# Attention loop of a fused convolution and attention kernel: the projection ahead before the transposes on PE, its conversion before the probabilities' copy on ACT

## What is computed

```python
q = hidden_states @ Wq                        # hidden_states: 8 images, 256 tokens, 128
k, v = jnp.split(hidden_states @ Wkv, 2, axis=-1)
scores = jnp.einsum('bqhd,bkhd->bhqk', q * scale, k).astype(jnp.bfloat16)
probs = jax.nn.softmax(scores, axis=-1)
out = jnp.einsum('bhqk,bkhd->bqhd', probs.astype(jnp.float32), v)
out = out.astype(jnp.bfloat16)
return out.reshape(B, S, H * dh).astype(jnp.float32) @ Wo + bo
```

## Time and profile before

| what | value |
|---|---|
| time, median of 3 runs | 681.39 us (680.37 to 681.64) |
| the profiled execution's own time | 678.21 us |
| its span on the core | 676.3 us |
| the changed loop | from about 376 to 508 us of the span |
| PE, DVE, ACT busy over the span | 91%, 80%, 59% |
| copy_out to copy_out, images 1 to 5 | 15.82 us each |

### The profile page before, as it was taken

The page is one execution under the profiler, slowest core; times in us unless marked ns, Lnnn a source line. Parts: engine busy times, 40 slices in busy tenths (PEclk is TensorE's granted clock), DMA queues, the critical chain, the costliest instruction groups (busy, mean ns, idle before and its releaser), DMA issues. The chain is left out here.

```text
span 676.3 us, 10078 instructions
## 1 busy us (share of the span) xinstructions
PE 614.9 (91%) x3226; PEld 486.4 (72%) x3226; DVE 541.3 (80%) x1150; ACT 401.6 (59%) x787; POOL 148.0 (22%) x114
## 2 busy tenths in 40 slices
PE   6998987997899999999997899999857799999996
PEld 4784665885678888887886778777746578888784
DVE  2638479975778778878788799999969589999986
ACT  3522221003678888888884799899953545555552
POOL 0095055754511001111011121111103011111200
PEclk9699586998899999999999555555558889999998
DMA  4000000002042211221000000000001232222200
GB/s 178 1 0 1 0 1 0 1 1 64 7 153 93 95 33 61 93 93 54 9 1 0 1 2 1 0 0 0 1 0 47 86 109 79 103 82 88 95 33 31
DMA packets 9699, 28.78 MB, mean 43 GB/s; under 512 B 960, under 2 KB 3264, under 8 KB 9536
## 3 DMA queue, kind: packets, MB, share of 16 engines
q1 hardware_dynamic: 9664, 28.34, 12.1%
HBM read 27.15 MB, written 1.18 MB: 42 GB/s over the span
## 5 line engine op out<-in xcount | busy, mean ns | idle before, releaser
L1249 DVE TENSOR_TENSOR hL<-hraw,hH 128x1024 fp32r<-128x1024 f32 (+1 forms) x128 | 131.1, 1050 | 35.9 <-ACT hH L1009 35.2
L1083 PE MATMUL ps<-xH,wH 128*128 128x512 f32 x256 | 103.7, 405 | 1.8 <-DVE xL L1154 1.1
L1013 ACT ACTIVATE hraw<-ps,bias 128x512 f32<-128x512 f32 x128 | 86.5, 685 | 28.8 <-PE ps L1085 24.4
L1085 PE MATMUL ps<-xH,wL 128*128 128x512 f32 x256 | 102.8, 402 | 0.0
L1084 PE MATMUL ps<-xL,wH 128*128 128x512 f32 x256 | 102.8, 401 | 0.0
L944 POOL TENSOR_TENSOR wL<-wraw,wH 128x1024 fp32r<-128x1024 f32 (+1 forms) x16 | 36.4, 2274 | 237.6 <-DVE wH L1135 237.6
L1097 PE MATMUL ps<-hH,wH 128*128 128x512 f32 x192 | 76.5, 398 | 7.5 <-DVE hL L1249 7.5
L1099 PE MATMUL ps<-hH,wL 128*128 128x512 f32 x192 | 76.2, 397 | 0.0
L1098 PE MATMUL ps<-hL,wH 128*128 128x512 f32 x192 | 75.9, 395 | 0.0
L1018 ACT ACTIVATE hraw<-ps 128x512 f32<-128x512 f32 x64 | 38.3, 599 | 52.0 <-PE ps L1085 50.4
L1009 ACT ACTIVATE hH<-hraw 128x1024 fp32r<-128x1024 f32 x64 | 67.5, 1055 | 1.0
(11 more groups left out here) (238 smaller groups left out, 1210.6 us busy)
## 6 DMA issues: line engine op xcount, KB each, us to landing
G<-gates_scratch SPq DMA_DIRECT2D x32, 512.0 KB, 4.7
wraw<-in_ex SPq DMA_DIRECT2D x8, 514.5 KB, 5.8
wraw<-in_ex SPq DMA_DIRECT2D x8, 384.0 KB, 5.1
w<-in_pack SPq DMA_DIRECT2D x1, 1420.5 KB, 8.1
xs<-in_x SPq DMA_DIRECT2D x4, 256.0 KB, 4.7
out<-acc SPq DMA_DIRECT2D x4, 256.0 KB, 2.1
w<-in_pack SPq DMA_DIRECT2D x1, 501.0 KB, 3.7
gates_scratch<-gT SPq DMA_DIRECT2D x4, 32.0 KB
```

The lines of the kernel that those rows point to most:

```text
L1013: act.activation(hraw[:, k % 2, h, :], ps[:, h, :], ACT.Gelu, bias=bias[:, place(k, last)[0], h:h + 1]).then_inc(z["act"], 1)
L1083: pe.matmul(o, wH[:, p, at:at + P], xa, start=True, stop=False)
L1085: x = pe.matmul(o, wL[:, p, at:at + P], xa, start=False, stop=True)
L1249: dve.tensor_tensor(hL[:, k % 2, g * half:(g + 1) * half, :], src, hi.bitcast(F32), ALU.subtract).then_inc(z["hl"], 1)
```

## The change

On PE, `project` now stands before `transposed` in each step; on ACT, `upper` now stands before `evacuate`. What is issued, and every wait, stays as it was.

```diff
@@ -1408,10 +1408,10 @@
             def step(b, g, first):
                 if there(*ahead(b, g, 2)):
                     rounded(*ahead(b, g, 2))
+                if there(*fragment(b, g, 5)[:2]):
+                    upper(*fragment(b, g, 5))
                 if g != 3 and not (first and g == 0):
                     evacuate(*((b, g - 1) if g else (b - 1, 3)))
-                if there(*fragment(b, g, 5)[:2]):
-                    upper(*fragment(b, g, 5))
                 if there(*ahead(b, g, 1)):
                     exponentials(*ahead(b, g, 1))
@@ -1548,9 +1548,9 @@
                 if g == 2 and not first:
                     final(b - 1)
-                transposed(b, g)
                 if there(*fragment(b, g, 6)[:2]):
                     project(*fragment(b, g, 6))
+                transposed(b, g)
```

## The result

The changed kernel takes 688.2 us (median of 4 runs, 686.85 to 691.12), the kernel before 681.09 in the same comparison. The ratio is 1.0117, with a 95% interval of 1.0085 to 1.015: 8.0 us slower by the ratio, between 5.8 and 10.2, and 7.1 us between the two medians. The forecast was 687.5.

A forecast was written before the change was run, and what follows sets the result against it. DVE was taken to bound the looped images, and the new order to make a longer cycle. Image 0 (1.15), four periods (4.12) and a fifth (0.8) gave 6.1 us, on 681.39 making 687.5 us, range 684.4 to 690.

The forecast's parts named there:

- upper bound of 17.07: Looped images: longest period forecast, in us, with every possible register-row cost added to 16.45.
- the cycle: Looped images: chain from `copy_out` through `lower`, projection, transposes, ACT's copies and value product to `copy_out`, 16.85 us against 15.82.
- unknown part of the register rows: Late starts at the projection and PE's other value product: cost shown by no row, half of it taken, 0.21 us.
- What bounds the kernel before: Looped images: DVE sets the pace, with a period of 15.82 us filled by its own work.
- DVE's own stretch: DVE from `copy_out` to the end of the image's last `lower`: 8.46 us without a wait, durations as before.
- The register rows: PE's instructions between a wait and the first matmul: 0.19 us more at the looped value product, taken as certain.
- The beginning: Loop's start: `lower`'s 3.51 us wait shortens by 0.88 us, but late first copies spend that gain.
- 1.1 us of slack: Kernel before, from the transposes to DVE: lateness that the queues of ACT and PE could absorb, about 1.1 us.
- rival 1: Looped images: DVE stays the bound and the lateness is covered; 680.5 to 681.4 us, no change; chance 0.06.
- the clock stood at half in the loop: Against the rival that PE's clock returns to 2.4 GHz in the loop, giving 679 us; chance 0.05.
- the register rows cost less, not more, than was taken: Against the rival that some four late starts a period cost 0.4 us each, giving 690.5 to 693; chance 0.08.
- rival 4: Looped images: half covered, as DVE's own copy path takes up part of the lateness; 682.8 to 684.4 us; chance 0.04.

The follow-up runs named there:

- e4: Kernel before, with POOL's value split started after the division of two steps before the image, not after its first scores' rounding; ratio to before 0.9998.
- e5: Changed kernel, with `lower` ahead of `normalise` on DVE; ratio to the kernel before 1.0067.
- e6: Changed kernel, with `copy_out` on DVE moved behind `centre` in an image's third step; ratio to the kernel before 1.0055.
- e3: Changed kernel, with POOL's value split started after the division of two steps before the image, not after its first scores' rounding; ratio to the kernel before 1.0058.
- e1: Changed kernel with ACT's old order restored, so only PE's projection stands ahead of the transposes; ratio to the kernel before 1.0086.
- e2: Kernel before with only ACT's half of the change, the conversion ahead of the copy; ratio to before 1.0093.

## Why the prediction was right

The sign and the mechanism came out, and so did the size by the timed medians (+7.1 for +6.1). By the loop the forecast was too low: the periods of 17.18 to 17.30 us lie above its upper bound of 17.07, and 8.0 us above its 7.4. That the median of the changed kernel came within 0.7 us of 687.5 is in part luck, since its four runs go from 686.85 to 691.12. Two terms of the sum were off, in opposite directions. Along the cycle, with the times of the period shown above:

| piece | forecast | measured |
|---|---|---|
| DVE, `copy_out` to the end of the last `lower` | 8.46 | 430.45 + 0.42 - 421.75 = 9.12 |
| hand-over and projection | 0.06 + 0.91 | 431.74 - 430.87 = 0.87 |
| transposes and hand-over | 1.03 + 0.06 | 432.94 - 431.74 = 1.20 |
| ACT, copy to copy | 3.82 | 436.77 - 432.94 = 3.83 |
| copy, hand-over with register rows | 1.02 + 0.06 + 0.19 | 438.03 - 436.77 = 1.26 |
| value product | 0.60 | 438.63 - 438.03 = 0.60 |
| output's transposes, hand-over | 0.37 + 0.06 | 439.05 - 438.63 = 0.42 |
| unknown part of the register rows | 0.21 | none |
| sum | 16.85 | 17.30 |

- *What bounds the kernel before*: DVE, and it does; e4 shows it, where POOL's 0.47 us became 0.30 + 0.05 and the period 0.12 shorter.
- *The cycle*: apart from DVE's own stretch and the unknown part, each piece is within 0.11 us. That ACT's path from copy to copy is the one that counts, and not PE's beside it, held too: ACT reaches the second copy, at 436.77, without a wait. e5 and e6 each take a piece out of the cycle, and the period falls.
- *The register rows*: at the value product nearly all of the 0.19 us was there (the copy ends at 437.80, the product starts at 438.03, 0.23 us later). At the projection it was not: `lower` ended at 430.87 and the projection started at 430.93. Half of a bound was taken for a cost that no row showed, and at the projection it is zero.
- *DVE's own stretch* was taken as unchanged, "8.46 us without a wait". It grew by 0.66 us although nothing on DVE was edited, because POOL's value split held more of it. This is the step that failed, a term that the sum did not have; e3 shows its size. The prediction asked of ACT's half only by how much the conversion delays the copy, not what else on ACT moves against the rest; the last section shows that POOL's start does.
- *The beginning*: `lower`'s first wait fell from 3.51 to 2.59 us, 0.92 against 0.88 forecast, and the gain was spent as I took it. DVE's timeline of the changed kernel there:

```profile
386.29 0.42 DVE L1568 SCALAR_TENSOR_TENSOR q3L<-ps,q3H 128x256 fp32r<-128x256 f32 x1 [2.59 <-ACT q3H L1367]
...
390.18 0.48 DVE L1570 SCALAR_TENSOR_TENSOR k3S<-k3H,w,ps 128x256 fp32r<-128x256 f32 x1 [0.30 <-ACT k3H L1367]
391.65 0.56 DVE L1604 TENSOR_REDUCE o3b<-ps 128x128 bf16<-128x384 f32 x1 [0.99 <-PE ps L1479]
...
395.70 0.42 DVE L1568 SCALAR_TENSOR_TENSOR q3L<-ps,q3H 128x256 fp32r<-128x256 f32 x1
```

  The next `lower` waits 0.30 and `gather` 0.99 us, and a later `lower`, at 395.70, stands 29.07 us behind the prologue's, 29.12 before.
- *The sum*: 1.27 + 5.69 + 0.92 + 0.13 = 8.0 us (image 0, four periods, the fifth, the end) against 1.15 + 4.12 + 0.8 + 0. The median of the timed runs, at +7.1, lies nearer to the forecast of +6.1 than the loop does; the interval of the ratio holds both.
- *Readings that were off*: the "1.1 us of slack" don't come out of the rows. From the transposes' end the chain could at best have reached `copy_out` at 430.33 + 0.06 + 1.02 + 0.06 + 0.60 + 0.37 + 0.06 = 432.50, and it came at 433.31: 0.8 us in all. The 1.1 us enter rival 1, not the sum. The last projection still stands in the second step of image 6 (at 481.36 us before), where the prediction has none left. `copy_out` waits 0.29 to 0.54 us in images 1 to 5, where "0.4 us or more each time" was forecast, and DVE is busy 94.04 us of the 100 from 400 to 500 us, where it was to be less than 94%.

The rivals fell: DVE did not stay the bound, the clock stood at half in the loop, the register rows cost less, not more, than was taken, and +7.1 us is past what rival 4, half covered, allows.

## What to carry to other kernels

Where an engine is full, count the slack of the whole chain to each hand-over before moving a step that it doesn't run: here there were 0.8 us from the transposes to `copy_out`, and by the prediction's rows the transposes came 1.3 us later. A step that waits must not be put in front of one whose operands are ready, unless the wait is known to be over; here each half did that, on PE with the wait for `lower`, on ACT with that for the projection. And when a delay enters a loop, look again at which engines now work side by side: 3.2 of 8.0 us lost were not a wait but slower work on an engine that was not touched.

## What the runs showed that was not expected: POOL's work holds DVE's

In the kernel before, POOL's first piece starts 0.26 us behind DVE's subtraction (434.68); in the changed one 0.04. With a window narrow enough to hold single instructions, the timeline of DVE before has one of the four subtractions and one of the four divisions:

```profile
434.88 0.28 DVE L1581 TENSOR_SCALAR s<-s,mx 128x256 bf16<-128x256 bf16 x1
...
435.81 0.49 DVE L1589 TENSOR_SCALAR p<-p,sm 128x256 bf16<-128x256 bf16 x1
```

and POOL before:

```profile
434.94 0.48 POOL L1346 CAST vp<-v3f 128x256 bf16<-128x256 f32 x1 [13.20 <-ACT s L1375]
435.50 0.73 POOL L1348 TENSOR_TENSOR v3r<-v3f,vp 128x256 f32<-128x256 f32 x1
```

The division takes 0.49 us where one alone takes 0.28, and it ends at 436.30, 0.07 behind POOL's, which runs from 435.50 to 436.23. In the changed kernel, DVE's first subtraction and two of the divisions:

```profile
423.13 0.51 DVE L1581 TENSOR_SCALAR s<-s,mx 128x256 bf16<-128x256 bf16 x1
...
424.77 0.96 DVE L1589 TENSOR_SCALAR p<-p,sm 128x256 bf16<-128x256 bf16 x2
```

and POOL:

```profile
423.17 0.40 POOL L1346 CAST vp<-v3f 128x256 bf16<-128x256 f32 x1 [14.83 <-ACT s L1375]
...
424.98 0.67 POOL L1352 TENSOR_TENSOR vp<-v3r,vp 128x256 bf16<-128x256 f32 x1
```

The subtraction begins before POOL's first piece and ends at 423.64, 0.07 behind the end of that piece. The divisions end at 425.73, 0.08 behind the end of the last piece, 425.65. In these rows, then, an instruction of these two kinds that begins while one of POOL's runs, or 0.01 to 0.04 us before it, is held until POOL's is done. One that begins a little earlier isn't: the subtraction at 434.88 is 0.06 us ahead of POOL's first piece and takes its 0.28 us beside it. What it costs depends on where the instructions begin, not only on how much of POOL's 2.5 us lies beside them, and that is why 0.2 us of shift could double the cost (0.47 us an image before, and in e1 too; 1.0 to 1.1 in the changed kernel and in e2).

The 0.2 us come from ACT's half of the change. POOL is released by ACT's rounding of the next image's first scores. In the changed kernel that rounding ends at 440.43 and POOL starts at 440.50:

```profile
439.41 1.02 ACT L1375 ACTIVATE s<-ps 128x1024 bf16<-128x1024 f32 x1
```

It starts 2.64 us after the copy at 436.77, and 2.63 us after it in e2. With ACT's old order the conversion, 0.26 us, stands between the copy and this rounding: 2.90 us in the kernel before (430.95 to 433.85), 2.92 in e1. DVE's subtraction comes 3.7 us after the start of that copy in all four. So POOL starts 0.26 and 0.32 us behind the subtraction with the old order, 0.04 to 0.07 with the new one. DVE's wait at `copy_out` is not what moves it: it is longest in e1, 0.5 us, where POOL's overlap is as small as before.

In e4 the maximum is held too (0.72 for 0.42 us), while the reduction beside POOL has its 0.69, as elsewhere. That agrees with the Trainium skill, Advanced Engine Details and Errata, GPSIMD Details, by which POOL shares a read and a write interface with DVE and conflicts with its two-port modes and with instructions that have two inputs in SBUF: the maximum has two inputs, the reduction one. That the subtraction and the division run in such a mode is shown by no row here.
